# The last batch's layer behind attention moves from Pool and ScalarE to VectorE, its folded rows go to another buffer, and the slots are redone

## The chip, the cores and the metric

The kernel runs on one core of a Trainium2 chip. A core has five engines that run their own instruction streams and meet through semaphores: TensorE (PE, matmuls into PSUM), VectorE (DVE), ScalarE (ACT), GpSimd (POOL) and SyncE (SP, which here only issues DMAs). The metric is the device time of one execution in microseconds. Below, "the median of the runs" is that of three runs; the profile is of one further execution.

## The reference, cut to what matters

The input x has 8 x 512 rows of 256, the context 8 x 1024 rows of 192. In short:

```python
# x + tanh(g) * xattn(layernorm(x), ctx): per batch of 512 rows, 4 heads
scores = einsum(Q, K) / sqrt(32)                 # 512 x 1024 for each head
topv, topi = top_k(scores, 32); probs = softmax(topv)
c_t = mean over heads of scattered probs @ V     # 512 x 256
scale_in, shift_in = split(c_t @ W_film_in + b)
x = layernorm(x_text) * (1 + 0.5*scale_in) + 0.5*shift_in
y = irfft(rfft(x, 2L) * Kf)[:L] + x * D_skip     # s4d, over time, per channel
scale_out, shift_out = split(c_t @ W_film_out + b)
xt = x_text + y * (1 + 0.5*scale_out) + 0.5*shift_out
xt = xt + gelu(layernorm(xt) @ W1 + b1) @ W2 + b2        # 256 -> 1024 -> 256
return layernorm(xt)
# x + tanh(g) * moe(layernorm(x)): 8 experts 256 -> 512 -> 256, top 1
logits = x @ gate_w; score = sigmoid(max(logits)); e = argmax(logits)
y = silu(xs @ rt_gate[e]) * (xs @ rt_up[e]) @ rt_down[e] # xs = x * score
out = y + silu(x @ sh_gate) * (x @ sh_up) @ sh_down      # shared expert
```

Everything is float32.

## The kernel before

The work is laid out in 8 batches (B = 8) of 512 rows, each four tiles of 128 rows. For one batch, attention is 16 pieces (4 row tiles x 4 heads; n counts them over all batches, 0 to 127). Per piece TensorE forms 128 x 1024 scores (L1792), VectorE finds the 32nd largest by four rounds of MAX8 and three of MATCH_REPLACE8 (L1452 to L1464, two pieces share it alternately), ScalarE takes exponentials (L1049), and Pool multiplies by the kept mask (`ee` by `tk`, L771 or L773) and adds into the sum over heads `acc` (L775). When the fourth head's sum is done, TensorE's `finish` steps transpose `acc` and form the context vector.

What the diff calls `post(b)` is the layer behind attention for batch b: FILM_IN (four products, c_t by the folded weights, with an own matmul of 128 and one of 65 rows), the fold (the sum and the difference of the upper and the lower half of the 512 rows, on Pool), DFT (four blocks), the product with the spectrum (two multiplications on DVE, a subtraction and an addition on Pool), INV (two blocks), FILM_OUT (four products; ScalarE or DVE copies, Pool multiplies and adds), layer norm statistics on DVE, root on ScalarE with Newton steps on Pool, TURN (transposes), UP (8 banks with gelu), DOWN (4), a norm without division over gout and bout on Pool (L902 to L907), residual add, another norm, TURN2, GATE, routing, the shared expert (SHARED, SH_DOWN).

Behind it, rows are routed: they are scattered to DRAM by expert (Pool's L930) and taken back in tiles of 128 rows of one expert. There are NJ = 39 such tiles. 21 of them (`tiles()`, T_TURN, T_GATE, T_UP, T_DOWN) run between the work of batches 4 to 7, the last four, 17 to 20, inside the last batch's `post`. Their rows are loaded by SP at L675, their weights at L680 to L689, and their outputs are added to DRAM by Pool at L1013. The last 18 (`routed()`, L2191 and L2201) run at the very end, when all expert weights lie in SBUF; `expert(e)` on SP loads these in 3 DMAs of 512 KB each.

What sets the order: each engine's program is one list made by `weave`. Every generator yields a slot, a number in the frame of its batch (`post_at(b)`, some 160 a batch); the smallest slot is emitted next. The slots are the tables POOL_..., ACT_..., DVE_..., PE_..., SP_...; an index `[b == B - 1]` picks the second row of a table for the last batch. A second effect is on PSUM: the four banks of the ring are given out in the order of TensorE's slots. `keep_warm` adds matmuls that compute nothing needed (L1770, the FILL tables) in front of a step. Waits are semaphores in the code, so a step that comes early in an engine's list holds back all behind it.

Names that the prediction uses: `xt` holds the folded rows, then the result of the inverse, and at the end of the batch the shared expert's output, which Pool's L937 adds to `out` in DRAM (s_acc counts those DMAs); `u` the layer's input; `xln` normalised rows (two buffers); `big` a 128 x 8 x 512 buffer; `tmp` four row tiles that also feed the scatter; L843 is Pool's subtraction that makes the low part of the keys for the next batch's scores, and L636 and L638 are the loads that it feeds, on SP.

## Time and profile before

| | |
|---|---|
| median of the runs | 1743.46 us (1742.68 to 1745.92, 3 runs) |
| the profiled execution | 1737.76 us, its span 1735.6 us |
| mean granted TensorE clock | 0.959 |
| PE busy | 1535.6 us, 88% |
| DVE busy | 1350.4 us, 78% |
| POOL busy | 1195.9 us, 69% |
| ACT busy | 1146.9 us, 66% |
| weights of 21 tiles and 8 experts, xs, stores | 115.27 MB by DMA, 66 GB/s mean |

The span runs from the first to the last instruction on the core. The share of busy time is an average: from 160 to 1460 us the kernel does attention with everything else beside it, and from 1460 us only the last batch's layer and tiles are left. The chain of work that ended last is followed back from the last instruction, to what released each step. TensorE's float32 matmul shows as two records, so "x4" on it is two matmuls.

### The profile page before, as it was taken

The numbers are of one execution on the slowest core, as the hardware profiler recorded it, in microseconds if no ns is written. First come the engines' busy times: TensorE is split into PE (matmuls) and PEld (weight loads), VectorE is DVE, ScalarE is ACT, GpSimd is POOL, SyncE is SP. The second block draws the span as 40 slices with busy tenths as digits, with TensorE's granted clock in tenths as the row PEclk, the third lists the DMA queues.
The fourth block names the chain that finished last, engine by engine and source line by source line (L and its number), as shares of the span: only waits on it lengthen the run. The fifth ranks groups of instructions, "written<-read, shape, count | busy, mean of one in ns | idle before, by whom it ended". The sixth has DMA issues, their size and how long they took to land.

```text
span 1735.6 us, 22438 instructions
## 1 busy us (share of the span) xinstructions
PE 1535.6 (88%) x7358; PEld 1135.2 (65%) x7369; DVE 1350.4 (78%) x2168; ACT 1146.9 (66%) x2101; POOL 1195.9 (69%) x1341
## 2 busy tenths in 40 slices
PE   4878868898889898889998999899989998999996
PEld 2456546665656565667686767676767776767896
DVE  5798799988998898978888888888888995111321
ACT  2388875686678658765887588757876687134442
POOL 1388775858876786788678876897689858633422
PEclk9899889998998999899999999999999999999999
DMA  7210031002200210123322331333132211842431
GB/s 199 54 34 4 20 104 31 13 19 61 43 13 25 64 35 13 36 74 95 95 73 62 76 94 51 76 82 98 46 80 65 86 32 40 266 143 88 95 50 22
DMA packets 97223, 115.27 MB, mean 66 GB/s; under 512 B 17840, under 2 KB 74168, under 8 KB 96964
## 3 DMA queue, kind: packets, MB, share of 16 engines
q1 hardware_dynamic: 85348, 100.32, 19.9%
q0 software_dynamic: 11760, 13.52, 5.2%
q8 instruction: 59, 0.97, 0.2%
q14 instruction: 56, 0.46, 0.1%
HBM read 75.48 MB, written 19.58 MB: 55 GB/s over the span
## 4 chain that ended last, share of the span: by engine, by line
PE 31%; DVE 28%; POOL 16%; ACT 16%; issue 7%; DMA 2%; SPq 1%; POOLq 0%; DVEq 0%
DVE R L1460 9%; DVE ZB L1464 7%; POOL ZB L773 4%; PE PS L2191 4%; DVE ZB L1456 4%; ACT ZB L1049 3%; PE PS L2039 3%; PE PS L1770 3%; PE PS L2068 2%; DVE R L1452 2%; ACT R L1052 2%; ACT R L1055 2%; PE PS L1820 2%; POOL ZB L775 2%; PE PS L2027 2%
## 5 line engine op out<-in xcount | busy, mean ns | idle before, releaser
L1460 DVE MAX8 R<-ZB 128x8 f32<-128x1024 f32 x384 | 471.1, 1227 | 10.9
L1770 PE MATMUL PS<-R 128*128 128x256 f32 x1118 | 290.4, 394 | 26.0 <-ACT R L1052 14.6
L1464 DVE MATCH_REPLACE8 ZB<-R,ZB 128x1024 f32<-128x1024 f32 x256 | 309.5, 1209 | 0.0
L773 POOL TENSOR_TENSOR ZB<-ZB 128x1024 f32<-128x1024 f32 x96 | 231.7, 2414 | 68.4 <-ACT ZB L1049 68.2
L1052 ACT ACTIVATE R<-PS 128x512 f32<-128x512 f32 (+6 forms) x404 | 173.3, 467 | 143.2 <-PE PS L2039 47.3
L1770 PEld LDWEIGHTS PS<-R 128*128 128x128 f32 x1118 | 211.2, 198 | 72.7 <-ACT R L1052 24.2
L775 POOL TENSOR_TENSOR ZB<-ZB 128x1024 f32<-128x1024 f32 x96 | 226.6, 2360 | 7.5
L1452 DVE MAX8 R<-PS 128x8 f32<-128x1024 f32 x128 | 155.9, 1218 | 6.9 <-PE PS L1793 6.9
L1456 DVE MATCH_REPLACE8 ZB<-R,PS 128x1024 f32<-128x1024 f32 x128 | 155.5, 1215 | 0.0
L1049 ACT ACTIVATE ZB<-ZB,R 128x1024 f32<-128x1024 f32 x128 | 147.1, 1149 | 4.2
L1049 ACT ACTIVATE ZB<-PS,R 128x1024 f32<-128x1024 f32 x128 | 141.6, 1106 | 3.1 <-DVE R L1472 2.8
L1049 ACT ACTIVATE R<-R 128x32 f32<-128x32 f32 (+2 forms) x356 | 96.6, 272 | 71.0 <-DVE R L1460 40.0
L771 POOL TENSOR_TENSOR ZB<-ZB 128x1024 f32<-128x1024 f32 x32 | 77.2, 2413 | 94.7 <-ACT ZB L1049 94.7
L1091 ACT ACTIVATE ZB<-PS,R 128x1024 f32<-128x1024 f32 x128 | 141.0, 1101 | 0.0
L1820 PE MATMUL PS<-ZB 128*128 128x193 f32 x512 | 105.3, 365 | 21.0 <-ACT ZB L1052 9.8
L2068 PE MATMUL PS<-R 128*128 128x512 f32 x256 | 116.2, 597 | 6.2 <-ACT R L1052 3.6
L2133 PE MATMUL PS<-R 128*128 128x512 f32 x256 | 121.1, 608 | 0.0
L1820 PEld LDWEIGHTS PS<-ZB 128*128 128x128 f32 x512 | 97.4, 215 | 32.3 <-issue 17.7
L2078 PE MATMUL PS<-R 128*128 128x256 f32 x512 | 116.4, 380 | 0.8 <-ACT R L1306 0.8
L2078 PEld LDWEIGHTS PS<-R 128*128 128x128 f32 x512 | 95.3, 189 | 16.0 <-ACT R L1306 1.0
L1045 ACT ACT_TABLE_LOAD x61 | 78.3, 1283 | 36.2 <-DVE R L1429 24.5
L1792 PE MATMUL PS<-ZR 97*128 97x512 f32 x128 | 80.7, 631 | 11.0 <-ACT ZB L1091 11.0
(256 smaller groups left out, 3150.1 us busy)
## 6 DMA issues: line engine op xcount, KB each, us to landing
ZR<-ZR SPq DMA_DIRECT2D x96, 128.0 KB
ZB<-in_L_ffn_rt_gate SPq DMA_DIRECT2D x21, 512.0 KB
ZB<-in_L_ffn_rt_up SPq DMA_DIRECT2D x21, 512.0 KB
ZB<-in_L_ffn_rt_down SPq DMA_DIRECT2D x21, 512.0 KB, 5.9
R<-in_x SPq DMA_DIRECT2D x16, 512.0 KB, 3.9
ZB<-in_ctx SPq DMA_DIRECT2D x8, 768.0 KB, 4.8
R<-xs_d SPq DMA_DIRECT2D x39, 128.5 KB, 2.1
out<-R SPq DMA_DIRECT2D x32, 128.0 KB, 3.7
```

Of the source, the lines that this page charges most:

```text
L773: pool.tensor_tensor(e, e, w, ALU.mult).then_inc(s.g_att, 1)
L775: pool.tensor_tensor(acc, acc, e, ALU.add).then_inc(s.g_att, 1)
L1049: return act.activation(*x, **k)
L1052: return act.activation(o, i, ACT.Copy, **k)
L1452: vec.max(ml[:, 0:8], sc_bank(n)).then_inc(s_tk[n % 2], 1)
L1456: vec.match_replace(w, ml[:, 0:8], sc_bank(n), NEG).then_inc(s_tk[n % 2], 1)
L1460: vec.max(ml[:, 8 * r:8 * r + 8], w).then_inc(s_tk[n % 2], 1)
L1464: vec.match_replace(w, ml[:, 8 * r:8 * r + 8], w, NEG).then_inc(s_tk[n % 2], 1)
L1770: pe.matmul(q_bank(*key)[:, 0:256], ident, warm, start=True, stop=True)
L1820: ins = pe.matmul(q_bank("finish", t, 2)[:, 0:CW], att[:, g, :], cb[b % 2][:, g, :], start=g == 0, stop=g == 7)
L2068: ins = pe.matmul(q_bank("post", b, UP + k), w1[:, c, k * 128:(k + 1) * 128], tr_post[:, c, :], start=c == 0, stop=c == 1)
L2078: ins = pe.matmul(q_bank("post", b, DOWN + i)[:, 0:256], big[:, k, i * 128:(i + 1) * 128], w2[:, k, :], start=k == 0, stop=k == 7 and b == ...
```

## The change

For the last batch (b = 7) the steps of `post` that ran on Pool and partly on ScalarE are written out for VectorE in a generator `close()`. Pool keeps the casts of row numbers, the scatter and the accumulating DMAs; ScalarE keeps the roots, one transposed copy of two, gelu, and copies both halves of FILM_OUT. The product of the last attention piece and its sum (n = 127) go from Pool to VectorE (`last_sum`). The folded rows go to `folded`, a buffer of `xln`, in place of `xt`, so the wait for the accumulating DMAs of batch 6 stands before the inverse's result. On TensorE FILM_OUT of the last batch is a generator of its own with slots ahead of DFT, and takes the layer's normalised input as a third matmul. `expert(1)` also waits for the inverse. All slot tables and FILL tables have new numbers.

```diff
-POOL_LOW = (106.1, 74.5, 76.5)
...
+POOL_LOW = (105.1, 75.4, 76.7)
...
+DVE_CLOSE = (92.3, 93.8, 91.5, 55.6, -107.1, -89.4, 104.4, 15, -286.3, 76, -103.8, 10.9, 111.7, 106.3, -20.2, 102.7, 60.6,
+          -305, -253.4, 113.9, 119.1, -23.9)
...
+        folded, scale_out = xln[B % 2], tr_prep.rearrange("p a (b n) -> p (a b) n", n=256)
...
-                on.wait_ge(s.g_att, 28 * B)
+                on.wait_ge(s.v_last, 2)
...
+                on.wait_ge(*q_run("post", B - 1, INV + 1))
...
-                for n in range(16 * B):
+                for n in range(16 * B - 1):
...
+                b, at = B - 1, post_at(B - 1)
+                yield at + POOL_ROUTE[1][1]
+                for i in range(4):
+                    on.wait_ge(*q_done("post", b, DOWN + i))
+                for i in range(4):
+                    pool.tensor_copy(tmp[i][:, D:XW].bitcast(U32), C["tok"][:, 4 * b + i:4 * b + i + 1]).then_inc(s.g_tok, 1)
...
+                            own.then_inc(copy(scale_out[:, i, :], bank[:, 0:256]))
+                            copy(xl[:, i, :], bank[:, 256:512]).then_inc(q_sem("post", b, FILM_OUT + i), 1)
...
+                        yield at + ACT_ROOT[1][1]
+                        v, r, y, ve = root_stats(st_post[1], False)
+                        on.wait_ge(s.v_mv, 8 * b + 8)
+                        root(v, r, y).then_inc(s.a_rs, 1)
...
+                    on.wait_ge(s.a_sg, b + 1)
+                    TS(sg, sg, 1.0, None, ALU.add).then_inc(s.g_sg, 1)
+                    on.wait_ge(s.g_sg, b + 1)
...
+                if b == B - 1:
+                    on.wait_ge(s.v_rc, b + 1)
+                    on.wait_ge(*q_run("post", b, TURN2 + 1))
+                    for i in range(4):
+                        TS(tmp[i][:, 0:D], tmp[i][:, 0:D], sg[:, i:i + 1], None, ALU.mult).then_inc(s.g_sx, 1)
...
+            def newton_last(q, shift):
+                m, v = by_vector(q)
+                r, y = q[:, 32:36], q[:, 40:44]
+                own.then_inc(TT(y, r, r, ALU.mult))
+                chain(STT, y, v, EPS, y, ALU.add, ALU.mult)
+                chain(TS, y, y, -0.5, 1.5, ALU.mult, ALU.add)
+                chain(TT, r, r, y, ALU.mult)
+                if shift:
+                    chain(STT, q[:, 36:40], m, -1.0, r, ALU.mult, ALU.mult)
+                on.wait_ge(own.sem, own.n)
+
+            def last_sum():
+                n = 16 * B - 1
+                t, e = n // 4, ee[n % 2]
+                yield tile_at(n) + DVE_CLOSE[0]
+                on.wait_ge(s.a_att, 5 * n + 5)
+                TT(e, e, tk[n % 2], ALU.mult).then_inc(s.v_last, 1)
+                on.wait_ge(s.g_att, 7 * t + 5)
+                on.wait_ge(s.v_last, 1)
+                TT(acc, acc, e, ALU.add).then_inc(s.v_last, 1)
+
+            def close():
+                b, n, at, xl = B - 1, 4 * B - 4, post_at(B - 1), xln[(B - 1) % 2]
+                q, q2 = st_post
+
+                def pair(x, i):
+                    return x.rearrange("p (a b) n -> p b a n", a=2)[:, i, :, :]
+
+                for i in range(4):
+                    yield at + DVE_CLOSE[1 + i]
+                    bank = q_bank("post", b, FILM_IN + i)
+                    on.wait_ge(*q_run("post", b, FILM_IN + i))
...
+                    own.then_inc(STT(u[:, i, :], bank[:, 0:256], rin[b % 2][:, i:i + 1], xl[:, i, :], ALU.mult, ALU.mult))
+                    on.wait_ge(own.sem, own.n)
+                    TT(u[:, i, :], u[:, i, :], bank[:, 256:512], ALU.add).then_inc(q_sem("post", b, FILM_IN + i), 1)
+                yield at + DVE_CLOSE[5]
+                for i in range(4):
+                    on.wait_ge(*q_done("post", b, FILM_IN + i))
+                on.wait_ge(s.g_fi, 4 * b)
+                on.wait_ge(*q_run("post", b - 1, FILM_OUT + 3))
+                own.then_inc(TT(folded[:, 0:2, :], u[:, 0:2, :], u[:, 2:4, :], ALU.add))
+                TT(folded[:, 2:4, :], u[:, 0:2, :], u[:, 2:4, :], ALU.subtract).then_inc(s.g_sd, 1)
+                for j in range(4):
+                    yield at + DVE_CLOSE[6 + j]
...
+                    spectrum(b, j, bank, q0, q1)
+                    on.wait_ge(own.sem, own.n)
+                    on.wait_ge(*q_done("post", b, DFT + j))
+                    own.then_inc(TT(yf[:, j, 0:256], q0[:, 0:256], q1[:, 256:512], ALU.subtract))
+                    TT(yf[:, j, 256:512], q0[:, 256:512], q1[:, 0:256], ALU.add).then_inc(s.g_y, 1)
+                for i in range(2):
+                    yield at + DVE_CLOSE[10 + i]
+                    bank = q_bank("post", b, INV + i)
+                    on.wait_ge(*q_run("post", b, INV + i))
+                    for k in range(4):
+                        on.wait_ge(s_acc[k], 16 * b)
+                    odd = qs[i][:, 0:256]
+                    chain(vec.tensor_copy, odd, bank[:, 256:512])
+                    on.wait_ge(own.sem, own.n)
+                    own.then_inc(TT(xt[:, i, :], bank[:, 0:256], odd, ALU.add))
+                    TT(xt[:, i + 2, :], bank[:, 0:256], odd, ALU.subtract).then_inc(q_sem("post", b, INV + i), 1)
+                    on.wait_ge(own.sem, own.n)
+                    on.wait_ge(*q_done("post", b, INV + i))
+                    for k in (i, i + 2):
+                        on.wait_ge(*q_done("post", b, FILM_OUT + k))
+                    chain(TT, pair(xt, i), pair(xt, i), pair(scale_out, i), ALU.mult)
+                    chain_to(s.g_fo, TT, pair(xt, i), pair(xt, i), pair(xl, i), ALU.add)
+                    on.wait_ge(s.g_fo, 4 * b + i + 1)
+                    for k in (i, i + 2):
+                        own.then_inc(vec.bn_stats(q[:, 6 * k:6 * k + 6], xt[:, k, :]))
+                on.wait_ge(own.sem, own.n)
+                for i in range(4):
+                    vec.bn_aggr(q[:, 24 + 2 * i:26 + 2 * i], q[:, 6 * i:6 * i + 6]).then_inc(s.v_mv, 1)
+                yield at + DVE_CLOSE[12]
+                on.wait_ge(s.v_mv, 8 * b + 4)
+                on.wait_ge(s.a_rs, 3 * b + 1)
+                newton_last(q, True)
+                for i in range(4):
+                    TS(tmp[i][:, 0:D], xt[:, i, :], q[:, 32 + i:33 + i], q[:, 36 + i:37 + i], ALU.mult, ALU.add).then_inc(s.a_ln, 1)
+                on.wait_ge(s.a_ln, 12 * b + 4)
+                biased = own.then_inc(TT(xt, xt, b2b.unsqueeze(1).broadcast_to([128, 4, 256]), ALU.add))
...
+                shifted = own.then_inc(TT(u, u, bout.unsqueeze(1).broadcast_to([128, 4, 256]), ALU.add))
+                for i in range(4):
+                    yield at + DVE_CLOSE[15 + i]
+                    on.wait_ge(*q_run("post", b, DOWN + i))
+                    on.wait_ge(own.sem, biased)
+                    TT(xt[:, i, :], q_bank("post", b, DOWN + i)[:, 0:256], xt[:, i, :], ALU.add).then_inc(q_sem("post", b, DOWN + i), 1)
+                    on.wait_ge(*q_done("post", b, DOWN + i))
+                    own.then_inc(vec.bn_stats(q2[:, 6 * i:6 * i + 6], xt[:, i, :]))
+                    on.wait_ge(own.sem, own.n)
+                    vec.bn_aggr(q2[:, 24 + 2 * i:26 + 2 * i], q2[:, 6 * i:6 * i + 6]).then_inc(s.v_mv, 1)
...
+                    chain_to(s.a_ln, STT, xt[:, i, :], xt[:, i, :], q2[:, 36 + i:37 + i], gout, ALU.add, ALU.mult)
+                yield at + DVE_CLOSE[19]
+                on.wait_ge(s.a_rs, 3 * b + 2)
+                newton_last(q2, False)
+                on.wait_ge(s.a_ln, 12 * b + 8)
+                on.wait_ge(own.sem, shifted)
+                for i in range(4):
+                    STT(x1[:, i, :], xt[:, i, :], q2[:, 32 + i:33 + i], u[:, i, :], ALU.mult, ALU.add).then_inc(s.g_z, 1)
+                for i in range(4):
...
+                    TS(tmp[i][:, 0:D], x1[:, i, :], q[:, 32 + i:33 + i], q[:, 36 + i:37 + i], ALU.mult, ALU.add).then_inc(s.a_ln, 1)
...
+                yield from route(b)
...
+                        on.wait_ge(*((s.g_att, 7 * t + 7) if t < 4 * B - 1 else (s.v_last, 2)))
...
+            def film_out(b):
+                for i in range(4):
+                    yield post_at(b) + POST_AT[b == B - 1][FILM_OUT + i]
+                    keep_warm(FILL_POST[b == B - 1][FILM_OUT + i], ("post", b, FILM_OUT + i))
+                    on.wait_ge(*q_done("finish", 4 * b + i, 3))
+                    bank, ins = film(b, FILM_OUT + i, i, 1, False)
+                    pe.matmul(bank[:, 256:512], ident, xln[b % 2][:, i, :], start=False, stop=True).then_inc(s.p_q, 1)
...
+                        both = xt if b < B - 1 else folded
...
-                        bank, ins = film(b, FILM_OUT + i, i, 1, b == B - 1)
-                        if b < B - 1:
-                            ins = pe.matmul(bank[:, 256:512], ident, xl[:, i, :], start=False, stop=True)
-                        ins.then_inc(s.p_q, 1)
+                    if b < B - 1:
+                        yield from film_out(b)
```

Three places of the order follow. In these rows a "x7" is seven more of the same, and the names in "waits" are semaphores; q0 to q3 are the four banks' rings.

TensorE, from the last FILM_IN products to the DFT. Before (L2001/L2002 FILM_IN, L2152/L2153 transposes of tile 17, L2163 its gate and up, L2027 DFT):

```order
L2001 MATMUL PS<-ZB,R 128x512 [waits q3]
L2002 MATMUL PS<-R 128x512
L2163 MATMUL PS<-R,ZB 128x128 [waits q0,q2,t_gu]
L2163 MATMUL PS<-R,ZB 128x128 x7
L1770 MATMUL PS<-R 128x256 [waits q1]
L1770 MATMUL PS<-R 128x256
L2163 MATMUL PS<-R,ZB 128x128 x8
L1770 MATMUL PS<-R 128x256
L2027 MATMUL PS<-R 128x256 [waits g_sd]
L2027 MATMUL PS<-R 128x256 x3
L2027 MATMUL PS<-R 128x256 [waits q3]
```

And now (L2175/L2176 a FILM product, L2185 its third matmul, so a FILM_OUT; L2331/L2332 tile 17's transposes, L2342 its gate and up, L2211 DFT):

```order
L2175 MATMUL PS<-ZB,R 128x512 [waits q3]
L2176 MATMUL PS<-R 128x512
L2331 MATMUL PS<-R 128x128 [waits q0,t_xs1]
L2332 MATMUL PS<-R 128x128
L2175 MATMUL PS<-ZB,R 128x512 [waits q1]
L2176 MATMUL PS<-R 128x512
L2185 MATMUL PS<-R 128x256
L2175 MATMUL PS<-ZB,R 128x512 [waits q2]
L2176 MATMUL PS<-R 128x512
L2342 MATMUL PS<-R,ZB 128x128 [waits q3,q0,t_gu]
L2342 MATMUL PS<-R,ZB 128x128 x15
L2211 MATMUL PS<-R 128x256 [waits q1,g_sd]
```

A FILM_OUT product with its third matmul now stands among the FILM_IN products; two more stand above the rows shown.

TensorE, from the DFT's end over the inverse. Before (L2172 tile 17's down product, L2039 the inverse, L2001/L2002 now FILM_OUT):

```order
L2172 MATMUL PS<-ZB,R 128x256 [waits q2,t_dn]
L2172 MATMUL PS<-ZB,R 128x256 x3
L1770 MATMUL PS<-R 128x256 [waits q3]
L1770 MATMUL PS<-R 128x256
L2039 MATMUL PS<-R 128x256 [waits g_y]
L2039 MATMUL PS<-R 128x256 x7
L2039 MATMUL PS<-R 128x256 [waits q0]
L2039 MATMUL PS<-R 128x256 x7
L2001 MATMUL PS<-ZB,R 128x512 [waits q1]
L2002 MATMUL PS<-R 128x512
```

And now (L2185 ends FILM_OUT's last product, L2351 tile 17's down product, L2223 the inverse, L2331/L2332 the transposes of tile 18's rows, t_xs0 the load of them, L2342 its gate and up):

```order
L2185 MATMUL PS<-R 128x256
L2351 MATMUL PS<-ZB,R 128x256 [waits q2,t_dn]
L2351 MATMUL PS<-ZB,R 128x256 x3
L2223 MATMUL PS<-R 128x256 [waits q3,g_y]
L2223 MATMUL PS<-R 128x256 x7
L2331 MATMUL PS<-R 128x128 [waits q0,t_xs0]
L2332 MATMUL PS<-R 128x128
L2223 MATMUL PS<-R 128x256 [waits q1]
L2223 MATMUL PS<-R 128x256 x7
L2342 MATMUL PS<-R,ZB 128x128 [waits q2,q0,t_gu]
L2342 MATMUL PS<-R,ZB 128x128 x7
```

Tile 18's transposes have come in between the two products of the inverse, and its gate and up products stand directly behind.

POOL, at the statistics of a batch's input and the keys of the next batch's second half. Before (L773/L775 product and sum over heads, L740 to L760 Newton steps, L843 the keys):

```order
L748 TENSOR_SCALAR R<-R 128x4 [waits g_own]
L740 TENSOR_TENSOR R<-R 128x4 [waits g_own]
L760 TENSOR_TENSOR R<-R 128x4 [waits g_own]
L843 TENSOR_TENSOR ZR<-R,ZR 128x512 [waits q0]
L773 TENSOR_TENSOR ZB<-ZB 128x1024 [waits a_att]
L775 TENSOR_TENSOR ZB<-ZB 128x1024 [waits g_att]
```

And now (L778/L780 product and sum, L745 to L765 Newton steps, L848 the keys):

```order
L753 TENSOR_SCALAR R<-R 128x4 [waits g_own]
L745 TENSOR_TENSOR R<-R 128x4 [waits g_own]
L765 TENSOR_TENSOR R<-R 128x4 [waits g_own]
L778 TENSOR_TENSOR ZB<-ZB 128x1024 [waits a_att]
L780 TENSOR_TENSOR ZB<-ZB 128x1024 [waits g_att]
L848 TENSOR_TENSOR ZR<-R,ZR 128x512 [waits q0]
```

The subtraction that feeds the key loads stands one product and one sum later.

## Rows read from the trace of the kernel before

**Rows 1.** the page: busy time of an engine, share of the span, instructions

```profile
PE 1535.6 (88%) x7358; PEld 1135.2 (65%) x7369; DVE 1350.4 (78%) x2168; ACT 1146.9 (66%) x2101; POOL 1195.9 (69%) x1341
```

**Rows 2.** windows: busy us (and count) by engine, granted clock, DMA share

```profile
160.00:1460.00 1300.00, 1170.30 (x5356) 854.53 (x5361) 1164.59 (x1801) 958.14 (x1815) 995.91 (x1112) 0.96 0.22 57
1460.00:1500.00 40.00, 33.48 (x149) 23.41 (x148) 1.24 (x4) 13.97 (x32) 33.44 (x57) 1.00 0.41 121
1500.00:1537.00 37.00, 35.93 (x160) 27.52 (x158) 11.02 (x27) 7.43 (x15) 20.19 (x33) 0.95 0.87 296
1537.00:1567.00 30.00, 29.60 (x105) 19.64 (x106) 1.67 (x4) 8.84 (x17) 3.20 (x2) 1.00 0.27 71
```

**Rows 3.** waits in 160 to 1460 us: in total, times, longest

```profile
DVE ZB L1456 <- POOL ZB L771: 47.0, 12, 4.5
...
DVE ZB L1456 <- POOL ZB L773: 16.2, 21, 1.5
```

**Rows 4.** the chain that ended last, to the DFT: start, us, what

```profile
1462.45 2.35 POOL ZB L775
...
1486.51 10.00 DMA out<-R
...
1499.21 8.89 PE PS L2027 x32
```

**Rows 5.** timeline at the first FILM_IN product: start, us, engine, what

```profile
1481.91 1.02 PE L2001 MATMUL PS<-ZB,R 128*128 128x512 f32 x2
```

**Rows 6.** groups by form on DVE: count, busy us, mean ns, idle before

```profile
L1464 DVE MATCH_REPLACE8 ZB<-R,ZB 128x1024 f32<-128x1024 f32 x256 | 309.5, 1209 | 0.0
...
L1626 DVE TENSOR_TENSOR R<-PS,R 128x512 f32<-128x512 f32 x32 | 21.9, 683 | 0.0
...
L1416 DVE SCALAR_TENSOR_TENSOR R<-R 128x256 f32<-128x256 f32 x26 | 12.2, 470 | 0.9
...
L1643 DVE TENSOR_TENSOR R<-PS,R 128x256 f32<-128x256 f32 x4 | 1.7, 426 | 33.9 <-PE PS L2078 33.9
```

**Rows 7.** the chain from the inverse to UP

```profile
1511.06 7.15 DMA out<-R
...
1526.74 2.07 PE PS L2163 x16
1528.83 0.60 ACT R L1380
1529.45 1.28 ACT L1045
...
1537.39 10.55 PE PS L2068 x24
```

**Rows 8.** DMA issues, 1480 to 1580 us: KB each, median us to landing

```profile
Z<-in_L_ffn_rt_gate SPq DMA_DIRECT2D x7, 512.0 KB, 10.4
```

**Rows 9.** DMA issues on the page: stores of the residual

```profile
out<-R SPq DMA_DIRECT2D x32, 128.0 KB, 3.7
```

**Rows 10.** the chain from the end of DOWN on

```profile
1566.61 0.44 DVE R L1643
...
1590.46 0.86 PE PS L1770 x4
...
1593.03 1.92 PE PS L2092 x16
...
1623.22 3.57 PE PS L2191 x32
```

**Rows 11.** groups by form on Pool, 1460 to 1600 us

```profile
L907 POOL TENSOR_TENSOR R<-R 128x256 f32<-128x256 f32 x4 | 2.7, 683 | 0.3
```

**Rows 12.** a window at the DFT's first products

```profile
1500.00:1504.00 4.00, 4.00 (x12) 3.23 (x11) 1.29 (x2) 0.00 (x0) 0.31 (x1) 0.58 1.06 371
```

**Rows 13.** line in 730 to 760 us: ns min/median/max, first, last start

```profile
L638 SPq DMA_DIRECT2D ZR<-mrow_d x4: 434/438/443, 737.4 to 744.3; - x4
```

**Rows 14.** the scores' matmuls in 728 to 765 us

```profile
L1792 PE MATMUL PS<-ZR x3: 471/527/797, 732.0 to 760.2; 97*128 97x512 f32 x3
```

487 lines of the change are left out of this document (265 added, 222 removed), and 20 rows, old and new, of tables (DVE_TOP, POST_AT).

## The prediction

> **What bounds the kernel now.** I read the page's busy table first, then the windows by stage, the waits, and last the chain that ended the run. DVE is busy for 78% of the span [rows 1], an average over two different stretches. From 160 to 1460 us PE is busy 1170 and DVE 1165 of 1300 us [rows 2]: attention, where VectorE picks the top 32 scores and Pool sums the heads. DVE's waits there that name Pool's products and sums are 47.0 and 16.2 us [rows 3]. From 1460 us on DVE is nearly idle: 1.2 of 40 us, 11.0 of 37, 1.7 of 30 [rows 2]. There the last batch's layer behind attention runs as one chain over TensorE, ScalarE, Pool and DMA, and from 1623.22 eighteen tiles run on TensorE, which nothing in the change touches. So the change moves work to the engine that has room. What counts is when four milestones of the chain come: the DFT at 1499.21 [rows 4], UP at 1537.39 [rows 7], the gate at 1593.03 and the last tiles at 1623.22 [rows 10].
>
> **First milestone, the DFT: 3.1 us earlier.** Two things stand ahead of it. (a) The last attention product and sum go from Pool to VectorE. Pool takes 2.35 us for one of 128x1024 [rows 4] and does its pairs one after the other; DVE's operations of that size take 1.21 [rows 6] and run beside Pool's pair before. Less one hand-over, the transposes and the shared expert's matmuls behind them start 3.3 us earlier. (b) The folded rows no longer overwrite the buffer that the previous batch's accumulating DMAs read. The last of these was issued at 1486.51 and took 10.00 us, and the DFT began 2.7 us behind it, at 1499.21 [rows 4]. Not all of this comes back. The change puts three of the four FILM_OUT products ahead of the DFT, and gives each a third matmul. Two matmuls of 128x256 take 0.86 us (four records of L1770 [rows 10]), so one takes 0.43, one of 128x512 twice that, and a product 0.86 + 0.86 + 0.43 = 2.15; three are 6.5 us. FILM_IN began at 1481.91 in before [rows 5] and would begin at 1478.6; four FILM_IN pairs (6.9), three FILM_OUT (6.5) and tile 17's gate and up (2 x 2.07 by [rows 7]) end at 1496.1. In-order work refills most of the hole that the DMA left, and the gain is about (a).
>
> **Second, UP: 1.5 us earlier (bounds 5.4 earlier, 1 later).** A block of the DFT costs DVE two products at 0.68 and now two operations of 128x256 at 0.43 to 0.47 [rows 6]: 2.3 us against TensorE's 8.89 / 4 = 2.2 [rows 4]. So the stage keeps its 9 us or a little more and the first INV product starts near 1507. Then a new wait: tile 18's transposes now stand between INV0 and INV1 on TensorE, and the tile's rows are loaded from DRAM on SP's queue behind 18 weight loads of 512 KB, the gate's half of which lands 10.4 us after its issue (median) [rows 8]. In before that load waited for tile 16's output DMA, issued at 1511.06 and 7.15 us long [rows 7], because Pool had its own steps ahead of it; that wait goes. Next in line is the queue of weight loads: its last one was issued near 1511.7 in before, now at 1508.4, so the tile's rows land 8 to 11 us later, at 1516 to 1519, and INV1 ends by 1520 to 1522.5. Without the transposes there it would end by 1514.5. Behind INV1 DVE needs a copy and two additions at 0.43, two operations of twice that size and the statistics, 3.6 us by [rows 6]. On ScalarE tile 18's silu (0.60) and copy now stand ahead of the root's table load (1.28 [rows 7]). With root, newton steps, norms and transposes, 5.5 us by the same rows, UP starts at 1534 to 1537.5; I take the middle, 1535.9. What the DFT gained is thus half given back, not added.
>
> The Trainium skill (DMA: Bandwidth & Descriptors, "Issuing engines are not separate DMA queues") says that transfers of SP and Pool run on the same 16 engines and interleave. The trace agrees: Pool's accumulating DMA took 10.00 us among the loads, where a plain store of 128 KB has a median of 3.7 [rows 9]. By that rule the tile's rows would see the backlog from any queue.
>
> **Third, the gate: 9 us more.** DOWN's end is T = 1566.6. From T to the gate pass 26.4 us [rows 10]: squares, a table load, Pool's newton steps, four applications, then twelve Pool operations of 0.683, 8.2 us [rows 11], statistics, a second root, and the matmuls of two tiles. In the change each row tile has on DVE an addition (0.43), statistics, a mean and a fused operation (0.47), three of the four under DOWN's matmuls; then a root, newton steps, four fused operations of 0.47 in place of the twelve, statistics, a root, newton, four norms: about 14 us with both roots, transposes and copy. That is no longer last. Tile 20's weights are issued when tile 19's up product is through (T + 4), land some 5 us later, its products take 4 (T + 13), its silu 0.60 stands ahead of the root on ScalarE, table load 1.28 and root 0.5 behind it, and a silu's successor on DVE ahead of newton; newton and norms 2.3 and transposes and copies 1.2 would put the gate at T + 18.4, of which 1 us overlaps since the up half is not needed by the silu: T + 17.4. So 26.4 - 17.4 = 9.0.
>
> **Behind the gate: 0.7 us (bounds 0 and 1.5).** 30.2 us pass there [rows 10]. Pool's four scalings move to DVE, but beside them lie the shared expert's matmuls, which set the time and stay.
>
> The tail: 1.5 + 9.0 + 0.7 = **11.2 us less** at the last tiles.
>
> **The attention stretch: 2.5 us less (bounds -12 and +14).** All slots are redone, yet in the order little moves: on Pool a first product falls behind 4-element operations and the key subtraction L843 behind one multiply/add pair; on DVE single products go a place later. 63 us of waits on Pool [rows 3] are what better slots can win from, a fifth of it, 12, at best. L843 comes 4.7 us later (2 x 2.35) in seven batches. In one batch's turn the loads fed by it were issued up to 744.3 us, the first head's near 737.4 [rows 13], and scores were issued at 732 and again from 749.6 to 760.2 [rows 14]: some 10 us between the first head's landing and its use, so 4.7 costs nothing there. Were it to cost 2 us in each of seven, that is +14. No row prices the other moves; I take -2.5, near zero.
>
> Sum: -13.7 us against the profiled execution's own 1737.76 (span 1735.6, 2.2 around it), so 1724.1. The median of the runs is 1743.46, 5.7 above that execution, so the forecast is 1743.46 - 13.7 = **1729.8 us**.
>
> **Rivals.**
> 1. A larger gain. Tile 18's rows land before INV0 ends (UP 5.4 earlier), and tile 20's weights are no bound (T to gate 14): 5.4 + 12.4 + 0.7, with 6 in attention, is 24.5: 1719. For it: DVE's own chain is that short. Against: the loads' 10 us [rows 8].
> 2. Moved in vain. TensorE idles 5 to 6 us for tile 18's rows and its clock falls. Behind the 2.7 us hole ahead of the DFT the granted clock was 0.58 for 4 us [rows 12], near the lower level (1.2 of 2.4 GHz): 4 x 0.42 = 1.7 us lost. Twice that behind two holes is 3.4; with rows landing at 1519 and tile 20's weights 3 us later the tail gains 4 to 5, and with +2 in attention the time is 1741: no change. For: both loads are on the busiest queue. Against: the holes replace one that cost the same.
> 3. Slower, by the key subtraction. In the batches with tiles (3 to 7) Pool is fuller than in the rows I read. If there the keys land less than 4.7 us ahead of the scores, scores come late and DVE, at 90%, never makes it up: up to 33 us over seven batches, +22 net, 1765; three full batches already make 14 - 11 = +3. It decides from a slack of 4.7 us down. Against: 10 us of slack in rows 13 and 14, and the pair goes earlier, which is what DVE waits for.
>
> The skill's page TensorE: Matmul & The Clock Gate ("HAM oscillation") has matmuls behind a wait for a DMA restart at half clock. The 0.58 agrees; by the rule the 16 matmuls of INV1 take up to 3 us more, which is rival 2's loss.
>
> **Chances.** Forecast 0.57, with its own range 1724 to 1736; rival 1 0.13; rival 2 0.15; rival 3 0.15, half of it mild. 0.2% (3.5 us) is about what a measurement of this kernel can tell from no change. Faster: 0.57 + 0.13 + 0.07 of rival 2 = 0.77; same 0.10; slower 0.13. The range that leaves about a tenth on each side is 1717 to 1745.
>
> **What would show it.** In the profile after: the DFT's first matmul at 1495 to 1498 with no DMA ahead of it in the chain; a hole of 4 to 8 us on TensorE before INV1, ended by the load of a tile's rows; UP at 1534 to 1537.5; T to gate 16 to 19 us with DVE in it and Pool absent; 29 to 30 us from the gate to the last tiles; DVE's waits on Pool in attention at 50 to 70 us. Wrong: keys as releaser of scores (rival 3); UP later than 1538; T to gate over 22; or the stretch to 1460 longer or shorter by over 6 us, which would lay the result on the slots, not on the moved work.

## The result, and the profile after

The changed kernel takes 1726.44 us (median of 7 runs, 1720.77 to 1728.94) against 1742.68 (7 runs, 1735.62 to 1745.92) for the kernel before on the same chip: a ratio of 0.9899, 95% interval 0.9879 to 0.9919. The forecast was 1729.8 us, faster, with a range of 1717 to 1745; the measured time is faster, inside the range and 3.4 us under the forecast. Several of its steps do not hold, as follows.

The page's busy line answers [rows 1]:

```profile
PE 1516.2 (88%) x7299; PEld 1122.8 (65%) x7307; DVE 1383.0 (80%) x2241; ACT 1136.6 (66%) x2069; POOL 1152.6 (67%) x1267
```

Pool gave up 43 us and DVE took 33. The windows (busy us and count on PE, PEld, DVE, ACT, POOL; granted clock; DMA share; GB/s), to be held against [rows 2]:

```profile
160.00:1460.00 1300.00, 1167.51 (x5312) 857.94 (x5315) 1156.95 (x1791) 954.03 (x1807) 992.48 (x1102) 0.96 0.22 57
...
1500.00:1530.00 30.00, 20.01 (x97) 16.44 (x96) 13.75 (x32) 1.92 (x5) 1.60 (x1) 0.83 0.91 313
```

Between 1500 and 1530 TensorE is busy 20 of 30 us and its granted clock is 0.83. The chain that ended last (start, us, what) shows why; it answers [rows 4, 7, 10]:

```profile
1461.05 3.35 DVE ZB L1737
1464.49 2.11 DVE ZB L1740
...
1469.12 2.86 PE PS L1995 x16
...
1484.73 1.89 SPq L693
1486.67 3.83 SPq L695
...
1511.10 8.61 DMA R<-xs_d
1519.76 0.47 PE PS L2331
...
1520.45 4.80 PE PS L2223 x16
...
1530.00 1.98 PE PS L2351 x8
...
1538.72 14.00 PE PS L2247 x32
...
1567.68 3.58 PE PS L2342 x32
1571.89 4.81 DMA ZB<-in_L_ffn_rt_up
1576.74 3.85 PE PS L2342 x32
...
1585.80 1.92 PE PS L2271 x16
...
1614.34 3.57 PE PS L2370 x32
```

Read it from the bottom. L2370 are the last tiles, L2271 the gate, L2247 UP. In the middle SP issues a row of weight loads (L693, L695), mostly 1 to 4 us each on its queue; behind them the load of tile 18's rows takes 8.61 us, and its transposes L2331 stand between the two products of the inverse, L2223. TensorE's timeline (start, us, line, operation, idle time before and its releaser; [rows 5] has the answering row of before) shows the same from the engine:

```profile
1478.97 1.02 PE L2175 MATMUL PS<-ZB,R 128*128 128x512 f32 x2
...
1496.11 7.09 PE L2211 MATMUL PS<-R 128*128 128x256 f32 x32
...
1506.91 3.62 PE L2223 MATMUL PS<-R 128*128 128x256 f32 x16
1519.76 0.47 PE L2331 MATMUL PS<-R 128*128 128x128 f32 x1 [9.23 <-DMA R<-xs_d]
...
1520.24 4.99 PE L2223 MATMUL PS<-R 128*128 128x256 f32 x16
```

The two profiled executions don't stand at the same place within their spreads, and attention ends elsewhere in each. So I set a zero where attention's work on DVE ends, at the start of its last top-k MAX8: 1458.6 in before, 1457.1 in after. From there:

| from the last MAX8 to | before | after | forecast of the step | measured step |
|---|---|---|---|---|
| first FILM_IN | 23.3 | 21.9 | | -1.4 |
| DFT | 40.6 | 39.0 | -3.1 | -1.6 |
| UP | 78.8 | 81.6 | -1.5 | +2.8 |
| end of DOWN, T | 108.0 | 110.6 | | |
| gate | 134.4 | 128.7 | -9.0 more | -8.3 more |
| last tiles | 164.6 | 157.2 | -0.7 more | -1.7 more |
| end of span | 277.0 | 269.5 | -11.2 | -7.5 |

The step behind the gate is less certain than it looks: the experiments show it to vary by 3.3 us with TensorE's clock alone (see e6).

The rest of the result lies ahead of the zero. Each profiled kernel gives a sample: with the new slots and the early start (after and seven of the experiments below, e1 to e5, e7, e8) the last MAX8 starts at 1448.1 to 1458.1, mean 1453.0; in the kernel before at 1458.6 and 1462.2, mean 1460.4. That is 7.4 us, where 2.5 was forecast. 7.4 and 7.5 are 14.9; the medians differ by 16.2.

Much of the scatter goes with the granted clock. From 160 to 1440 us it was 0.97 in e1, e2, e3, e5 and e8, whose last MAX8 starts at 1448.1 to 1453.1, and 0.95 to 0.96 in after, e4 and e7, where it starts at 1456.7 to 1458.1. The timed runs say the same: the fastest of the changed kernel's seven, 1720.77 us, had a clock of 0.958 over the whole run, the slowest, 1728.94, had 0.952. Whether the clock is the cause or follows from TensorE's waits is not shown.

DVE's waits in the attention stretch (in total, times, longest), against [rows 3]:

```profile
DVE R L1491 <- PE PS L1968: 26.9, 15, 6.6
DVE R L1514 <- ACT R L1075: 24.9, 19, 3.0
DVE ZB L1495 <- POOL ZB L776: 20.2, 5, 5.9
...
DVE ZB L1495 <- POOL ZB L778: 10.9, 13, 1.6
```

The kernel before has in the same stretch, beside [rows 3]:

```profile
DVE R L1475 <- ACT R L1049: 7.3, 12, 1.0
DVE R L1452 <- PE PS L1793: 5.3, 6, 1.1
```

Waits on Pool fell from 63 to 31 us (all of them are for its products; none names the sum). The wait for scores on TensorE (L1968) grew from 5.3 to 26.9 us, up to 6.6 at a time, and the wait for ScalarE's part of the softmax (L1514) from 7.3 to 24.9.

### The profile page after: what moved, and what is told of

It reads as the page before. It is cut to its first block, busy times and chain, and to the rows that moved or that the text cites. A ratio compares the mean times of both kernels' runs of the same rounds, so it can differ in the third digit from the quotient of the medians.

```text
span 1726.6 us, 22306 instructions
## 1 busy us (share of the span) xinstructions
PE 1516.2 (88%) x7299; PEld 1122.8 (65%) x7307; DVE 1383.0 (80%) x2241; ACT 1136.6 (66%) x2069; POOL 1152.6 (67%) x1267
## 4 chain that ended last, share of the span: by engine, by line
PE 35%; DVE 25%; ACT 16%; POOL 12%; issue 7%; DMA 2%; SPq 2%; POOLq 0%; DVEq 0%
DVE R L1499 7%; DVE ZB L1503 6%; PE PS L2370 4%; POOL ZB L778 3%; PE PS L2247 3%; PE PS L2223 3%; PE PS L1945 3%; DVE ZB L1495 3%; ACT ZB L1075 3%; PE PS L1995 3%; DVE R L1455 2%; ACT R L1081 2%; PE PS L2321 2%; DVE R L1491 2%; ACT ZB L1078 2%
## 5 line engine op out<-in xcount | busy, mean ns | idle before, releaser
L1499 DVE MAX8 R<-ZB 128x8 f32<-128x1024 f32 x384 | 470.9, 1226 | 10.3
L1945 PE MATMUL PS<-R 128*128 128x256 f32 x1048 | 279.6, 398 | 14.8 <-ACT R L1078 11.3
L778 POOL TENSOR_TENSOR ZB<-ZB 128x1024 f32<-128x1024 f32 x95 | 230.1, 2422 | 87.2 <-ACT ZB L1075 87.1
L1945 PEld LDWEIGHTS PS<-R 128*128 128x128 f32 x1048 | 199.3, 199 | 62.9 <-issue 17.7
L780 POOL TENSOR_TENSOR ZB<-ZB 128x1024 f32<-128x1024 f32 x95 | 224.2, 2360 | 7.4
L1491 DVE MAX8 R<-PS 128x8 f32<-128x1024 f32 x128 | 156.0, 1219 | 28.9 <-PE PS L1968 28.9
L2312 PE MATMUL PS<-R 128*128 128x512 f32 x256 | 123.7, 618 | 0.0
L1995 PE MATMUL PS<-ZB 128*128 128x193 f32 x512 | 103.5, 361 | 21.4 <-ACT R L1078 9.2
L2247 PE MATMUL PS<-R 128*128 128x512 f32 x256 | 117.1, 601 | 2.4 <-ACT R L1078 1.1
L2257 PE MATMUL PS<-R 128*128 128x256 f32 x512 | 116.2, 379 | 1.7 <-ACT R L1342 1.7
L1995 PEld LDWEIGHTS PS<-ZB 128*128 128x128 f32 x512 | 95.9, 212 | 31.9 <-issue 17.9
L2257 PEld LDWEIGHTS PS<-R 128*128 128x128 f32 x512 | 95.6, 189 | 16.7 <-issue 1.7
L1039 POOL DMA_INDIRECT out<-R x21 | 34.0, 1617 | 104.8 <-ACT R L1078 92.1
L1967 PE MATMUL PS<-ZR 97*128 97x512 f32 x128 | 77.4, 605 | 25.2 <-ACT ZB L1117 16.2
```

The source lines that it names most:

```text
L778: pool.tensor_tensor(e, e, w, ALU.mult).then_inc(s.g_att, 1)
L780: pool.tensor_tensor(acc, acc, e, ALU.add).then_inc(s.g_att, 1)
L1491: vec.max(ml[:, 0:8], sc_bank(n)).then_inc(s_tk[n % 2], 1)
L1499: vec.max(ml[:, 8 * r:8 * r + 8], w).then_inc(s_tk[n % 2], 1)
L1945: pe.matmul(q_bank(*key)[:, 0:256], ident, warm, start=True, stop=True)
L1995: ins = pe.matmul(q_bank("finish", t, 2)[:, 0:CW], att[:, g, :], cb[b % 2][:, g, :], start=g == 0, stop=g == 7)
```

## The experiments

**Is the time reproduced, and where does a run vary?** e6 is the kernel before, once more, with no edit.

> The kernel before, once more with a profile, to see what of its time is attention and what the last layer. In its first profile the last MAX8 started at 1458.6 and 277.0 us followed, but that execution was 5 us below its median; five executions of kernels with the changed kernel's attention had the last MAX8 at 1448.6 to 1458.1. Theory A (the changed slots shorten attention by 5 to 9 us, the last layer by 7.5): the last MAX8 starts at 1461 to 1466 and 277 us, within 0.5, follow. Rival B (attention is the same and the first profiles were typical): it starts at 1453 to 1459.

Measured: 1741.29 us, last MAX8 at 1462.2, tail 276.9. The tail repeats to 0.1 us, while the attention stretch moved by 3.6 us between two profiles of one kernel. So an attention effect needs several profiles or medians. In the kernels with the change the tail does not repeat so well, and it goes with the granted clock. From the gate to the last tiles TensorE runs the same instructions without a gap in all of them, and yet (windows of after, e7 and e4):

```profile
1585.80:1614.20 28.40, 28.40 (x107) 18.15 (x108) 14.82 (x52) 9.18 (x15) 12.34 (x15) 0.94 0.49 153
1586.45:1613.10 26.65, 26.65 (x106) 17.43 (x107) 14.87 (x52) 9.13 (x14) 12.34 (x16) 1.00 0.53 160
1587.10:1617.10 30.00, 30.00 (x106) 19.23 (x107) 14.82 (x52) 9.13 (x14) 12.34 (x15) 0.89 0.48 147
```

It is 26.7 us in e1, e7 and e8, 28.4 in after, e2 and e3, and 30.0 in e4, e5 and e10; times the clock each comes to 26.7. In the same way the eight matmuls of the context vector (L1995, 16 records) took 2.86 us in after, e2 and e7 and 4.53 in e1, e4 and e10, behind the same two short waits. A tail effect of 2 us or less must therefore be read step by step, between two points of the chain that the clock didn't touch. Such steps do repeat: from the first FILM_IN product to the DFT 17.1 us in each kernel with the change.

**The hole between the inverse's products.** e2 issues the tile's row load ahead of the weight loads:

```diff
-          90.4), (12, -361.4, -797.8), (32.7, 14.8, -70.2), (-24.5, 111, 55.5), ...
+          90.4), (12, -361.4, -797.8), (13, 13.2, 14.5), (-24.5, 111, 55.5), ...
+                    if e in (5, 7):
+                        yield post_at(B - 1) + (14 if e == 5 else 15)
```

The first line is tile 18's row of SP_TILE (rows, gate/up weights, down weights); the other two let the loads of experts 5 and 6 come behind its rows and gate/up weights, and those of expert 7 behind all three.

> The changed kernel with SP's list altered: tile 18's rows and its gate and up weights are loaded behind 9 of the 18 expert loads, its down weights behind 15, instead of all three behind 18. Theory A (the load queue is the whole hole): rows land at about 1504, before INV0 ends, no hole on TensorE ahead of INV1, INV1 ends at 1514, UP starts at 1529 to 1531, 8 to 10 us earlier than in the changed kernel, and the gate and the end of the run come 7 to 9 us earlier. Rival B (something else ends the wait, for instance the accumulating output DMA of tile 16 or the DMA bandwidth itself): the hole before INV1 stays over 4 us, or the gain turns up as a wait for tile 18's weights; UP at 1535 or later.

Measured: 1720.6 us (1714.1 to 1722.13), ratio to before 0.9871 (0.9843 to 0.9899), against 0.9899 for the change. The tail is 259.2, 10.3 less than in after, and UP starts 71.15 behind the last MAX8 instead of 81.65. Its chain:

```profile
1504.28 11.19 DMA ZB<-in_L_ffn_rt_down
1515.52 2.01 PE PS L2353 x8
...
1524.25 14.00 PE PS L2249 x32
```

The hole is gone (the inverse's two products run one behind the other), so it was real and cost 10 us in the tail of this execution; the next bound is tile 18's down weights, in the same queue. The timed runs show less of it: the median is 5.8 us under the changed kernel's of the first measurement, and the two intervals of the ratio overlap from 0.9879 to 0.9899. e8, below, has the same edit and is clear of that doubt.

e1 leaves SP alone and puts tile 18's transposes behind the inverse on TensorE:

```diff
-          95.4), (4.4, 8, 8.3, 14.7), (19.3, 24.4, 28.3, 29.2), (36.2, 64.3, ...
+          95.4), (4.4, 8, 8.3, 14.7), (24, 24.4, 28.3, 29.2), (36.2, 64.3, ...
```

> The changed kernel with one slot altered: tile 18's two transposes stand behind the second product of the inverse (INV1) on TensorE instead of in front of it; all else equal. Theory A (the wait for tile 18's rows, which held INV1 from 1510.5 to 1519.8, delayed the layer): INV1 runs at 1510.5 to 1514, the transposes wait until about 1519.7, and only tile 18's own silu and T_DOWN stand before the root; UP starts at about 1534 instead of 1538.7, span 4 to 5 us shorter than the changed kernel at the same clock. Rival B (the root waits for tile 18's silu and T_DOWN copy on ScalarE, so the layer gains nothing by itself): UP moves only by INV1's 5 us of TensorE time at most if tile 18's products start that much earlier, and not at all if its weights are late; under 1 us of the 4.7 are seen at the gate.

Measured: 1724.27 us (1716.32 to 1730.71), ratio 0.9891 (0.9844 to 0.9937), tail 267.6, 1.9 less. Its chain runs through the weights of the same tile:

```profile
1507.95 10.36 DMA ZB<-in_L_ffn_rt_up
1518.36 6.00 PE PS L2342 x32
```

By the timed runs that is no difference from the change. In the profile UP starts 57.8 us behind the first FILM_IN product instead of 59.7, so moving the waiting instruction back gains 2 of the 10 us, because the next step of tile 18 waits for the same backlog, then runs at a lower clock (6.00 us, 3.73 in after), and the root on ScalarE stands behind it. The load had to move, not the consumer.

**The last sum, and DVE beside Pool.** In after DVE's product and sum take 3.35 and 2.11 us in the chain. The groups by form say that an operation of that size takes 1.2 (columns: busy us, mean ns):

```profile
L1809 DVE TENSOR_TENSOR R<-R 128x1024 f32<-128x1024 f32 x1 | 1.2, 1227 | 0.0
```

Pool's timeline of after covers them:

```profile
1460.96 2.35 POOL L780 TENSOR_TENSOR ZB<-ZB 128x1024 f32<-128x1024 f32 x1
1463.26 4.46 POOL L972 TENSOR_TENSOR R<-R 128x512 f32<-128x512 f32 x2
1469.12 1.27 POOL L972 TENSOR_TENSOR R<-R 128x512 f32<-128x512 f32 x1 [1.40 <-ACT R L1078]
```

DVE's product began at 1461.05, 0.09 behind Pool's sum, and ended 1.07 behind the end of that sum; Pool's two L972 took 4.46 where one alone takes 1.27. e3 keeps the engines apart: DVE's product waits for Pool's sum of the pair before, and Pool's `shared()` of batch 6 waits for DVE's sum.

```diff
+                        if b == B - 2:
+                            on.wait_ge(s.v_last, 2)
...
+                on.wait_ge(s.g_att, 7 * t + 5)
                 TT(e, e, tk[n % 2], ALU.mult).then_inc(s.v_last, 1)
-                on.wait_ge(s.g_att, 7 * t + 5)
```

> The changed kernel; DVE's product of the last attention piece waits for Pool's last sum, and Pool's next product (shared expert of batch 6, 128x512) waits for DVE's sum, so that the two engines don't work on two SBUF inputs at the same time there. In the changed kernel DVE's product took 3.33 us and its sum 2.10, and Pool's two 128x512 products beside them 4.46 us together, where 1.22 and 1.27 each are their durations elsewhere. Theory A (they hold each other up at SBUF): product and sum take 1.2 us each and the Pool products 1.27 each; the transposes behind the sum start 0.5 to 1 us earlier, near 1466.0. Rival B (it is the 128x1024 operands in this buffer, or the engine's own doing): product and sum stay over 2 us alone, and the transposes start 2 us or more later.

Measured: 1719.56 us in a single run, tail 269.2. DVE's timeline of e3:

```profile
1454.96 1.23 DVE L1740 TENSOR_TENSOR ZB<-ZB 128x1024 f32<-128x1024 f32 x1 [4.49 <-POOL ZB L780]
1456.22 1.23 DVE L1742 TENSOR_TENSOR ZB<-ZB 128x1024 f32<-128x1024 f32 x1
```

Apart, both take 1.23 us. The start of the transposes behind them comes 9.0 us after the last MAX8 instead of 9.64: 0.6 us gained, for DVE now waits for what it had contended with.

The Trainium skill (SBUF — State Buffer, "SBUF: two separate sides") calls the port pair that VectorE and GpSimd share an exclusive lock, held for a whole instruction, also when a VectorE operation has two SBUF inputs and the GpSimd operation reads SBUF. The trace agrees within 0.2 us: 2.35 - 0.09 + 1.07 = 3.33, a wait for Pool's whole instruction and then a little less than one duration of its own (1.07 for 1.23).

e5 undoes the move of the sum: Pool does piece 127 again.

```diff
-                for n in range(16 * B - 1):
+                for n in range(16 * B):
-            weave(setup(), ..., shares(), last_sum(), prep(), ...)
+            weave(setup(), ..., shares(), prep(), ...)
```

The three waits for VectorE's sum become waits for Pool's again.

> The changed kernel with the product and the sum of the last attention piece back on Pool; all else of the change stays. Theory A (the prediction's term (a), corrected by the two engines' holding each other up): from the last MAX8 to the first FILM_IN product pass 22 us in the changed kernel; on Pool the pair adds 4.7 us behind Pool's pair before it but no longer slows it, so 25 us, 2 to 3.5 us more, and the DFT starts as much later. Since tile 18's rows queue behind loads that wait for the same sum, the shift passes on to the end: from the last MAX8 to the end 271.5 to 273 us instead of 269.5. Rival B (the sum is hidden by something else, for instance by the shared expert's products on ScalarE and Pool): under 1 us at FILM_IN.

Measured: 1724.03 us in a single run, tail 274.1, 4.6 more than after. (The time is under the change's median all the same, because attention ended early in this execution, at 1448.1.) TensorE's timeline of e5:

```profile
1459.16 1.61 PE L1986 MATMUL PS<-R,ZB 128*128 128x128 f32 x8 [2.26 <-POOL ZB L780]
1462.03 4.98 PE L1995 MATMUL PS<-ZB 128*128 128x193 f32 x16 [1.27 <-ACT R L1078]
```

The transposes start 11.1 us behind the last MAX8 (1448.1) instead of 9.64; in the kernel before it is 11.1 too. So the move is worth 1.4 us, not 3.3: beside Pool the two operations took 3.0 us more than 1.23 each, which is more than what is missing. FILM_IN starts 25.9 behind the zero instead of 21.9, over the 2 to 3.5 us that I expected, because the context products L1995 took 4.98 us instead of 2.86 at a granted clock of 0.57. That part can't be put down to the sum's place: e1, e4 and e10 have the sum on VectorE and took 4.53, and the kernel before has it on Pool and took 2.87. Against the kernel before FILM_IN came 1.4 us earlier (23.3 to 21.9).

**The folded rows' buffer.** e4 folds into `xt` again, behind the accumulating DMAs:

```diff
-        folded, scale_out = xln[B % 2], tr_prep.rearrange(...)
+        folded, scale_out = xt, tr_prep.rearrange(...)
+                for k in range(4):
+                    on.wait_ge(s_acc[k], 16 * b)
```

> The changed kernel with the folded rows of the last batch written to xt again, and so the wait for the four accumulating DMAs of batch 6 back in front of the fold on DVE; everything else of the change stays. Theory A (FILM_OUT and tile 17's products now fill TensorE until 1496.1, and the DMAs, issued from 1481.8 on, land by about 1495): the fold waits 1 to 3 us, the DFT starts at 1496 to 1499, and the gate moves by less than 1.5 us, since tile 18's rows hold INV1 until 1519.8 anyway; the time is within 0.2% of the changed kernel. Rival B (the new buffer is what brought the gain): the DFT starts at 1499 or later and the whole chain, the end included, comes 3 us or more later.

Measured: 1725.09 us (1721.82 to 1731.65), ratio 0.9888 (0.9857 to 0.9919): the same as after. The tail is 271.7, but its FILM_IN was already 1.7 late (its L1995 took 4.53 us), and from there to the DFT it takes 17.1 us as in after, so nothing of it is the buffer's. The forecast was a wait of 1 to 3 us; DVE's fold waited for nothing:

```profile
1496.72 0.69 DVE L1767 TENSOR_TENSOR R<-R 128x512 f32<-128x512 f32 x1 [0.29 <-DVE R L1759]
```

With three FILM_OUT products ahead of the DFT, the old DMAs are done before the fold wants the buffer.

**The key subtraction.** e7 puts Pool's subtraction (L848) back ahead of the product and sum:

```diff
-POOL_LOW = (105.1, 75.4, 76.7)
+POOL_LOW = (105.1, 75.4, 76.5)
```

> The changed kernel with the third key-low subtraction of every batch on Pool (L848) moved ahead of a first product and a product/sum pair, some 7 to 8 us earlier, as its only alteration. Theory A (the keys land 5 us or more ahead of the scores that use them also in the changed kernel): pieces 16 to 128 take the same time within the scatter of 3 us, and the time is within 0.3% of the changed kernel, or a little more, where Pool then waits for ScalarE ahead of it. Rival B (rival 3 of the prediction: the late keys cost attention time): DVE's waits for scores, 26.9 us in all in the changed kernel, fall by half or more, and the time falls by 5 us or more.

Measured: 1725.74 us (1723.52 to 1728.66), ratio 0.9904 (0.9888 to 0.992), the same as after. Its largest wait for scores:

```profile
DVE R L1491 <- PE PS L1968: 24.9, 13, 6.7
```

Pool's subtraction ran 11 to 15 us earlier from batch 1 on, and the waits stayed. So the subtraction's place is not what the scores wait for, and rival 3, which saw the loss there, is refuted.

The keys themselves are not cleared by this. The longest wait, 6.6 us up to 247.7, is for the first scores of batch 1 (the second of the eight), which also need the keys' load on SP. The timelines of after, SP and TensorE:

```profile
232.70 0.43 SPq L617 DMA_DIRECT2D R<-in_L_xattn_W  x1
233.23 3.13 SPq L640 DMA_DIRECT2D ZR<-ZR  x3
246.43 0.77 PE L1967 MATMUL PS<-ZR 97*128 97x512 f32 x1 [7.54 <-issue]
```

By the landings in the trace head 0's keys (L640, issued from 233.23) are complete at 246.34, 0.09 us before the scores start; in e7 the distance is 0.09 as well. Two loads of 1024 KB each (L616 and L617, constants and weights for a later step) were issued right in front of them, at 232.22 and 232.70. In the kernel before these two were issued at 221.64 and 222.05, the keys from 248.68 on, and the keys were complete at 253.6: 4.9 us instead of 13.1. So in this one batch the new slots on SP made the keys late. In batches 2 to 7 head 0's keys are complete 4.6 to 12.0 us ahead of the scores (9.6 to 10.4 in the kernel before), and no score waits for them. No run moved the two loads back, so what this wait costs at the end is not measured.

**Where the 7 us of attention come from.** The first top-k MAX8 starts at 78.7 us in before (L1452) and 70.1 in after (L1491), so the stretch is early before it begins. TensorE's timeline of the kernel before shows a wait of 8.81 us at 19.64:

```profile
19.64 1.19 PE L1770 MATMUL PS<-R 128*128 128x256 f32 x2 [8.81 <-DMA R<-in_c_tri]
20.62 1.06 PE L1843 MATMUL PS<-R,ZB 128*64 128x128 f32 x4
21.61 0.31 PE L1776 MATMUL PS<-R 32*128 32x32 f32 x1
```

L1770 is `keep_warm`, a fill matmul that computes nothing needed. It read the constants up to the triangle and waited for the triangle's load; the real transposes, and DVE's set-up chain from 21.96 us on, queued behind it. The change makes it read columns that come with an earlier load, and with FILL_PREP's new numbers no fill stands there at all. In after the transposes L2018 run at 11.29 us. e9 is the kernel before with only that read and wait changed (the order of every engine is the same):

```diff
-        warm = R[:, alloc.top:alloc.top + 256]
+        warm = R[:, 0:256]
-                    on.wait_ge(s.ld_tri, 16)
+                    on.wait_ge(s.ld_cst, 16)
```

> The kernel before with one thing changed: the filling matmuls (L1770) read the constants' columns 0 to 255 and wait for the constants' load instead of that of the triangle, so that the two of them that stand early in the first preparation no longer hold TensorE until 19.64 us. The order of all engines stays as it is. Theory A (this one wait is what shortened the attention stretch): DVE's first copy of the set-up starts at 12 to 14 us instead of 21.96, its first top-k MAX8 near 70 instead of 78.73, and the last MAX8 comes 5 to 9 us earlier than the 1458.6 and 1462.2 of the kernel before, so at 1450 to 1456; the tail behind it stays at 277; time 1733 to 1738. Theory B (the new slots shortened it, and what the start gains is waited away again later): the start is early by 9 us all the same, but the last MAX8 stays at 1457 to 1463 and the time within 2 us of the kernel before.

Measured: 1736.12 us (1733.38 to 1740.59, 8 runs), before 1743.94, ratio 0.9963 (0.9941 to 0.9984). Its TensorE timeline:

```profile
9.97 1.06 PE L1770 MATMUL PS<-R 128*128 128x256 f32 x2
10.83 1.06 PE L1843 MATMUL PS<-R,ZB 128*64 128x128 f32 x4
11.82 0.31 PE L1776 MATMUL PS<-R 32*128 32x32 f32 x1
```

The last MAX8 starts at 1454.8, the tail is 276.9, unchanged. e10 puts the wait for the triangle back into the changed kernel, ahead of L2018's transposes:

```diff
+                    on.wait_ge(s.ld_tri, 16)
```

> The changed kernel with one wait put back: the first preparation's second group of transposes on TensorE (L2018) waits for the load of the triangle, as TensorE did in the kernel before. Nothing else is touched. Theory A: DVE's first copy starts near 21 to 23 us instead of 12.63, its first top-k MAX8 near 79 instead of 70.11, the last MAX8 comes 5 to 9 us later than the mean of 1453.0 of the kernels with the new slots, so at 1458 to 1462, and the time is 1731 to 1735 against 1726.4. Theory B: the last MAX8 stays at 1448 to 1458 and the time at 1724 to 1729.

Measured: 1736.29 us (1729.99 to 1740.24, 7 runs), ratio 0.9951 (0.9929 to 0.9973), so 0.52% or 9 us more than the change (0.9899). The timeline of e10:

```profile
20.17 1.06 PE L2019 MATMUL PS<-R,ZB 128*64 128x128 f32 x4 [8.39 <-DMA R<-in_c_tri]
```

The last MAX8 starts at 1458.4, the tail is 271.9: of the 9 us some 2 lie in the tail, where L1995 and the stretch behind the gate had the lower clock; the time is 1.3 us over the 1731 to 1735 expected. Taking the wait out and putting it in both move the first MAX8 by 8 to 9 us (from 79.0 on average to 70.2 in e9, from 69.0 to 76.6 in e10) and the last one by 5 to 8, so theory A holds from both sides. Following the first MAX8 of the n-th piece through the stretch (starts, us):

| n | before | e6 | e9 | after | e3 | e10 |
|---|---|---|---|---|---|---|
| 8 | 151.1 | 150.6 | 142.8 | 144.0 | 142.1 | 150.6 |
| 16 | 249.1 | 246.4 | 238.7 | 232.1 | 230.2 | 238.8 |
| 32 | 416.0 | 413.4 | 405.7 | 411.8 | 407.1 | 415.4 |
| 64 | 744.3 | 748.0 | 740.5 | 743.5 | 737.4 | 745.6 |
| 128 | 1450.8 | 1454.5 | 1447.0 | 1449.3 | 1440.9 | 1450.7 |

e9 keeps its 7.7 us on e6 from the 16th piece to the 128th (7.5): there the late start is never made up, and the granted clock from 160 to 1440 us was 0.95 in both. e10 lies 8 to 10 us behind e3 all along, at 0.97 in both; against after, which ran at 0.96, its lag shrinks from 6.6 us to 1.4. Beside this the new slots gain another 8 to 10 us up to piece 16 (e10 against before and e6) and have given them back at piece 32. From piece 16 to piece 32 DVE is idle for 23 us in after and for 11 in before, at the same busy time (157 and 156); 6.6 of the 12 us are the wait for batch 1's keys. Over the stretch e10 ends 2 us ahead of the mean of before and e6 (1452.6), less than those two differ.

**The fastest version tried.** e8 takes both edits, e2's and e3's.

> Both alterations of the second and third run together: tile 18's loads ahead of the last expert loads, and the last sum on DVE apart from Pool's products. Theory A (they are independent): from the last MAX8 to the end 258.5 to 259.5 us (269.5 in the changed kernel), the time 0.5 to 0.7% below the changed kernel, ratio to before about 0.983. Rival B (the second run's profile gained more than its timed runs show, because a shorter tail is paid for elsewhere): ratio to before 0.987 or more.

Measured: 1709.32 us (1709.28 to 1715.02) against 1742.23, ratio 0.9823 (0.9808 to 0.9837), tail 257.7; it is 1.8% faster than the kernel before and 0.8% faster than the change, clear of both intervals. Its last bound ahead of UP is the same as in e2:

```profile
1500.96 11.12 DMA ZB<-in_L_ffn_rt_down
1512.13 2.61 PE PS L2355 x8
```

## Why the prediction was right, and where it was not

**Right in sign and sum, by errors that cancelled.** -13.7 us was forecast, -16.2 measured. The tail gave 3.7 less than thought, attention 4.9 more. That the sum came within 2.5 us is luck: neither error was foreseen, and two of the signs that I had named as wrong appeared, UP later than 1538 and an attention stretch that is over 6 us shorter by the means.

**The DFT (forecast -3.1, measured -1.6).** The refill was worked out well: FILM_OUT and tile 17's gate and up filled the hole, 17.1 us from FILM_IN to the DFT where 17.5 was forecast, with no DMA ahead of it. (That the DFT began at 1496.11 to the digit of the forecast's 1496.1 is chance: attention ended 1.5 us earlier in this execution.) That the gain is term (a) and not the DMA's 10 us was right too (e4). Term (a) itself was mis-sized: 2.35 us on Pool against 1.21 on DVE left out that DVE's two operations would run beside Pool's own, and there they take 3.33 and 2.10. What remains is 1.4 us (e5).

**UP (forecast -1.5, measured +2.8; outside its bounds of -5.4 and +1).** The mechanism was as written: the load of tile 18's rows behind SP's weights, a hole on TensorE ended by it. The inverse began at 1506.91, as forecast (near 1507). Two sizes failed. The load was issued at 1511.10 and landed at 1519.71, past the late end of "1516 to 1519": issued 2.7 us later than the last weight load that I counted from, and 8.61 us long. With the inverse's first product ending at 1510.5 (1506.91 + 3.62) the hole is 9.2 us, not 4 to 8. And the second product ran partly at the lower clock and took 4.80 instead of 3.62, so the inverse ended at 1525.25 and not at 1520 to 1522.5. From there to UP it is 13.5 us, no longer than the 14 to 15 of the forecast. But the terms that I wrote out for it (3.6, 0.60, 1.28 and 5.5) make only 11.0; what the sum left unnamed is tile 18's down product (1.98) and its copy on ScalarE (0.39), which the chain shows ahead of the root. My own text named "UP later than 1538" as wrong, and it came at 1538.72. What I should have concluded from the rows is what e2 shows: this hole is a large item of the tail, 10 us, and it stands on the order of one queue.

**T to the gate (forecast 17.4 us, measured 18.1).** Right, and by the chain named: tile 20's weights (4.81 us from issue, forecast 5), its products, the root behind the silu, newton, norms on DVE; Pool is absent. It is 17.8 to 18.2 in all kernels with the change and 26.5 in the three without. (The terms as written make T + 18.9 and not T + 18.4; with that, 17.9.) **Behind the gate** 28.5 us for 29.5 forecast: 1.7 instead of 0.7 gained, just above the bound of 1.5. This says nothing of the moved scalings: the same code took 26.7 to 30.0 us by the clock, and the kernel before 30.0 at a clock of 0.89.

**Attention (forecast -2.5, measured -7.4).** This step failed by omission. "All slots are redone, yet in the order little moves" looked at products and keys, not at the fill matmuls, of which I priced no wait. The diff had the change of `keep_warm`'s operand and semaphore, and the timeline of before had its 8.81 us. The wait gives about 5 to 8 us (last MAX8 of e9 against before 5.6, by medians 7.8; of e10 against the new slots' mean 5.4, against the five at its clock 7.9), which is most of the 7.4. What the slots give by themselves is not shown: 2 us by e10, within the scatter of one kernel, so -2.5 for the slots alone is neither borne out nor refuted. DVE's waits on Pool fell by 32 us to 31, outside the forecast band of 50 to 70, but waits for scores (21.6 us more) and for ScalarE (17.6 more) took their place. The slack of some 10 us that I read for the keys was one batch's; in batch 1 of the kernel before it was 2.6 us.

**The rivals.** Rival 1 (rows early, 5.4 more at UP) did not occur, though its condition, created in e2, gives more than it said. Rival 2 described the tail half rightly: the hole for tile 18's rows cost 1.2 us more by the lower clock (on the eight matmuls of the inverse's second product, which show as the 16 records that I called matmuls), the gate kept its 8 us. (The hole on TensorE ahead of the DFT in the kernel before, from which I took its price, was 2.04 us; the 2.7 are counted from the DMA's landing.) Rival 3 is refuted by e7 as it stands, by the subtraction; its sign, keys as releaser of scores, appeared all the same in one batch, by the order of SP's loads. That the tail's gain could be doubled by the start was no case of mine.

**What stays open.** The new slots lose again between pieces 16 and 32 what they gain before; about half of the loss is the wait for batch 1's keys, the rest is not traced, and no run took it away. The attention stretch of the kernel before varies by 4 us and that of the new slots by 10; it goes with the granted clock, but what makes the clock differ between executions of one kernel is not shown. Nor is the gain of the slots alone, or of the scalings moved behind the gate.

## What to carry to other kernels

Read an engine's timeline from the first microsecond: an instruction that computes nothing needed can still wait, and when the engine behind it is bound for the whole run, most of its 8 us are still there at the end (e9, e10). When a step waits for a load behind a backlog, look up the position of the load in its queue before moving the step; moving the load gave 10 us of the tail (e2), moving the consumer 2 (e1). A load can also be held back by large ones that a new slot has put right in front of it (the keys of batch 1). An operation moved to the faster engine to run beside the slower one must be priced beside it, not from a row where it ran alone.

## What the runs showed of the hardware

- DVE's operations of 128x1024 with two SBUF inputs took 3.33 and 2.10 us beside Pool's and 1.23 apart; Pool's L972 took 2.2 each beside DVE's and 1.27 apart.
- After idle time TensorE was slower for the next matmuls in some executions: behind 9.2 us without work 16 records of L2223 took 4.80 us instead of 3.62. Behind two waits of 0.8 and 1.3 us, 16 records of L1995 took 4.53 us in e1, e4 and e10 (granted clock 0.62) and 2.86 in after, e2 and e7 (1.00), so a short wait may cost 1.7 us more than its length or nothing. In the window from 1500 to 1530 us the granted clock was 0.83, a mixture of its two levels, 1.2 and 2.4 GHz.
- The same matmuls from the gate to the last tiles, without idle time between them, took 26.7, 28.4 or 30.0 us at a granted clock of 1.00, 0.94 and 0.89.
- A small load behind SP's queue of 512 KB loads took 8.61 us from issue, and 512 KB of tile weights 10.36 to 11.19 there, but 4.81 at 1571.89, when the DMA share of the 7 us before was 0.00. Three key loads of 128 KB took 13.1 us from the first issue to the last landing right behind two loads of 1024 KB, and 4.9 without them.
